# A Mamba and mixture-of-experts layer: block 0's front over more PSUM banks, tables by stage, normalisation on ScalarE

## What is computed

```python
xn = (x - mean(x)) / sqrt(var(x) + 1e-5)
# state-space layer: E = 512 channels, N = 16 states
hidden, gate = split(xn @ W_in)
hidden = silu(conv4(hidden) + conv_bias)          # causal, depthwise
dt, B, C = split(hidden @ W_x)                    # 128, 16, 16 columns
dts = softplus(dt @ W_dt + b_dt)
state = exp(dts * A) * state + dts * B * hidden   # scan over the tokens
y = (sum_n(state * C) + hidden * D) * silu(gate)
out1 = y @ W_out
# experts: 32 of them with 96 columns, all computed, weighted by the top 8
rw = top8(softmax(xn @ router.T)), divided by its sum
out2 = sum_e((silu(xn @ w_gate[e]) * (xn @ w_up[e])) @ w_down[e] * rw[e])
out = x + out1 + out2
```

## Time and profile before

| | |
|---|---|
| median of 3 runs | 1367.48 us (1365.01 to 1369.09) |
| the profiled run | 1367.53 us, its span 1365.7 us |
| TensorE busy, products and weight loads | 1312.0 us (96%), 1233.5 us (90%) |
| VectorE busy | 1242.2 us (91%) |
| ScalarE busy | 1193.1 us (87%) |
| GpSimd busy | 1243.7 us (91%) |
| mean granted TensorE clock | 0.995 |

### The profile page before, as it was taken

One profiled execution on the slowest core, in us unless ns is written; L12 is line 12 of the kernel. 1 busy time (PEld: TensorE's weight loads), 2 busy tenths in 40 slices (PEclk: granted clock), 3 DMA queues, 4 the chain that ended last, 5 costly groups with the idle time before them and its releaser, 6 DMA issues.

```text
span 1365.7 us, 26543 instructions
## 1 busy us (share of the span) xinstructions
PE 1312.0 (96%) x9314; PEld 1233.5 (90%) x9314; DVE 1242.2 (91%) x1644; ACT 1193.1 (87%) x1990; POOL 1243.7 (91%) x625
## 2 busy tenths in 40 slices
PE   2599999999999999999999999999999999999998
PEld 2589999999999999999999999999999999999987
DVE  4598989999899999999999899999989999998987
ACT  3889899889889988999899989989998999988984
POOL 2789999999989999999999999999999999999996
PEclk9899999999999999999999999999999999999999
DMA  6544344534434544444444434434443444434442
GB/s 167 153 133 122 118 130 126 129 115 128 128 113 127 140 121 122 127 119 122 124 125 129 123 114 123 144 115 129 121 124 115 130 131 127 121 119 118 124 133 70
DMA packets 184533, 170.76 MB, mean 125 GB/s; under 512 B 42672, under 2 KB 167632, under 8 KB 184400
## 3 DMA queue, kind: packets, MB, share of 16 engines
q1 hardware_dynamic: 150608, 121.86, 30.7%
q10 hardware_dynamic: 33792, 47.20, 12.1%
HBM read 163.72 MB, written 5.24 MB: 124 GB/s over the span
## 4 chain that ended last, share of the span: by engine, by line
PE 53%; DVE 16%; POOL 12%; ACT 9%; issue 9%; ACTq 1%; SPq 0%; DMA 0%; DVEq 0%; POOLq 0%
PE pair_ps L849 22%; PE out_ps L967 12%; PE front_ps L849 7%; POOL state L468 6%; DVE state L750 5%; PE turn_ps L929 5%; PE out_ps L977 3%; ACT decay L546 3%; DVE acc L757 3%; POOL state L477 3%; POOL moe L483 2%; DVE u L767 2%; ACT L546 2%; DVE dt L738 2%; DVE moe L774 1%
## 5 line engine op out<-in xcount | busy, mean ns | idle before, releaser
L750 DVE TENSOR_TENSOR_SCAN state<-decay,state 128x512 f32<-128x512 f32 x512 | 615.0, 1213 | 70.6 <-ACT decay L546 67.4
L468 POOL TENSOR_TENSOR state<-du,b_rep 128x1024 f32<-128x1024 f32 x256 | 639.2, 2505 | 29.0 <-DVE u L767 28.9
L546 ACT ACTIVATE decay<-dt,neg_a 128x255 f32<-128x255 f32 x1024 | 437.2, 467 | 39.6 <-DVE state L750 27.2
L967 PE MATMUL out_ps<-w_down,moe 128*128 128x256 f32 x1536 | 353.0, 379 | 0.1
L483 POOL TENSOR_TENSOR moe<-moe,rw_rep 128x512 f32<-128x512 f32 x192 | 285.9, 1492 | 45.8 <-DVE moe L774 36.5
L967 PEld LDWEIGHTS out_ps<-w_down,moe 128*128 128x128 f32 x1536 | 283.1, 190 | 34.6 <-issue 0.5
L849 PE MATMUL pair_ps<-xnT_hi,w_up_hi 128*128 128x256 f32 x768 | 228.7, 298 | 8.9 <-ACT moe L554 8.7
L477 POOL TENSOR_TENSOR state<-state,c_rep 128x1024 f32<-128x1024 f32 x96 | 228.6, 2382 | 2.7 <-DVE state L750 2.7
L546 ACT ACT_TABLE_LOAD x176 | 225.8, 1283 | 3.1
L849 PE MATMUL pair_ps<-xnT_hi,w_gate_hi 128*128 128x256 f32 x768 | 223.2, 291 | 0.6 <-DVE moe L774 0.5
L849 PE MATMUL pair_ps<-xnT_hi,w_up_lo 128*128 128x256 f32 x768 | 217.6, 283 | 0.0
(11 more groups left out here) (112 smaller groups left out, 2055.2 us busy)
## 6 DMA issues: line engine op xcount, KB each, us to landing
w_down<-in_L_ffn_w_down_dram SPq DMA_DIRECT2D x384, 128.0 KB, 2.6
b_rep<-b_dram ACTq DMA_DIRECT2D x128, 256.0 KB, 3.4
rw_rep<-rw_dram SPq DMA_DIRECT2D x256, 96.0 KB, 2.6
rw_rep<-rw_dram SPq DMA_DIRECT2D x256, 64.0 KB, 2.7
c_rep<-b_dram ACTq DMA_DIRECT2D x96, 128.0 KB, 3.1
rw_rep<-rw_dram SPq DMA_DIRECT2D x256, 32.0 KB, 2.5
x_in<-L_attn_input_states_dram SPq DMA_DIRECT2D x16, 256.0 KB, 3.5
res<-L_attn_input_states_dram SPq DMA_DIRECT2D x16, 256.0 KB, 4.1
```

The costliest lines, as they stand in the source:

```text
L468: pool.tensor_tensor(state[:, n % STATES, :, :], du2[:, q, :, :], b_rep[:, n // BCH % 2, n % BCH, :][:, None, :].broadcast_to([P, ET, T]), ...
L546: last = act.activation(decay[:, h, j, 1:T], dt[:, q, e, 1:T], ACT.Exp, scale=neg_a[:, e, n:n + 1])
L750: dve.tensor_tensor_scan(x, decay[:, h, :, :].rearrange("p e t -> p (e t)"), x, 0.0, ALU.mult, ALU.add).then_inc(scanned, 1)
L967: last = pe.matmul(out_ps[:, c, :], moe[:, p % RING, j, c * P:(c + 1) * P], w_down[:, p % RING, j, :], start=(p == 0 and j == 0 and c == 0 ...
```

## The change

Five things are altered together.

1. In block 0 the front's products are spread: `hid1`, `lowT` and `dt1` go to the first half of `turn_ps`, `logits` and `weightsT` to the second; both are idle before the first scan. `hid1` then no longer waits for `taps0`, nor `dt1` for ScalarE's reading of `dt0`. The router's two steps are no longer in `FRONT` and have semaphores of their own in all blocks. In block 0 `low` doesn't wait for them; in the others it still waits for `weights_read`.
2. `w_in` is split by columns, the hidden half as split 0, the gate half as split 13. `hid0` waits for split 0 alone.
3. The tables have three stages: block 0, blocks 1 to 14, and block 15.
4. VectorE's `normed` becomes one small instruction, `shift` = -mean * rstd, and two passes of ScalarE (`normed`, Identity with scale and bias). A wait is added: ScalarE's `normed` for `shift_ready`.
5. The last product of `route` (weights divided by their sum) becomes `share`, two passes of ScalarE, which wait for `rw_step`.

The diff also lets VectorE take some of GpSimd's `weigh` and `state_output` steps, but the lists that choose them are empty; these steps keep their engine, and their semaphores are renamed.

```diff
-    FRONT = ["xnT", "hid0", "hid1", "logits", "weightsT", "low", "lowT", "dt0", "dt1"]
-    BY_SCALAR = [name for name in FRONT if name not in ("xnT", "logits")]
+    FRONT = ["xnT", "hid0", "hid1", "low", "lowT", "dt0", "dt1"]
+    ROUTER = ["logits", "weightsT"]
+    BY_SCALAR = FRONT[1:]
...
-    PE_FRONT = {'xnT': -112, 'hid0': -106, 'hid1': -99, 'logits': -90, 'weightsT': -59, 'low': -56, 'lowT': -46, 'dt0': -44, 'dt1': -24}
-    SILU_AT = [-4, 13, 26, 36, 44, 55, 62, 73, 94, 94, 113, 113]
-    SCALAR_FRONT = {'xnT': -115, 'hid0': -108, 'hid1': -93, 'weightsT': -64, 'low': -54, 'lowT': -51, 'dt0': -40, 'dt1': -29}
-    CONV_SILU_AT, ROUTER_EXP_AT, SOFTPLUS_AT, FIRST_AT, SKIP_AT = [-66, -71, -22, 6, 18]
+    def stage(i):
+        return 0 if i == 0 else 2 if i == BLOCKS - 1 else 1
+    UNIT_AT = [[-30, -19, -12, -11, -8, 16, 23, 31, 36, 48, 55, 60, 66, 66, 76, 78, 85, 90, 103, 103, 107, 110, 122, 123],
+               [2, 4, 8, 17, 19, 21, 27, 44, 45, 47, 48, 65, 65, 71, 72, 84, 85, 85, 104, 106, 110, 112, 120, 120],
+               [-5, 1, 10, 26, 27, 28, 37, 37, 43, 46, 55, 55, 65, 65, 69, 69, 84, 97, 101, 115, 142, 144, 165, 175]]
+    PE_FRONT = [{'xnT': -126, 'hid0': -118, 'hid1': -99, 'logits': -95, 'weightsT': -14, 'low': -68, 'lowT': -57, 'dt0': -56, 'dt1': -39},
+                {'xnT': -112, 'hid0': -111, 'hid1': -102, 'logits': -87, 'weightsT': -52, 'low': -49, 'lowT': -46, 'dt0': -42, 'dt1': -29},
...
+    SILU_AT = [[-14, -13, 20, 28, 37, 52, 65, 67, 97, 99, 116, 116],
+               [-1, 14, 24, 39, 46, 55, 60, 73, 96, 97, 116, 119],
+               [-3, 27, 36, 37, 57, 59, 69, 70, 85, 93, 130, 232]]
+    SCALAR_FRONT = [{'xnT': -119, 'hid0': -116, 'hid1': -100, 'weightsT': -9, 'low': -76, 'lowT': -74, 'dt0': -58, 'dt1': -55},
...
+    SCALAR_ALONE = [{'conv_silu': -84, 'router_exp': -79, 'softplus': -20, 'first_state': 14, 'skip': 7, 'normed': -120, 'share': -17},
+                    {'conv_silu': -75, 'router_exp': -81, 'softplus': -22, 'first_state': 7, 'skip': 20, 'normed': -124, 'share': -63},
+                    {'conv_silu': -82, 'router_exp': -80, 'softplus': -19, 'first_state': 6, 'skip': 16, 'normed': -123, 'share': -68}]
...
+    VECTOR_ALONE = [{'stats': -121, 'lo': -87, 'logits': -54, 'route': -48, 'taps0': -61, 'taps1': -57, 'total': 163, 'shift': -118},
+                    {'stats': -126, 'lo': -107, 'logits': -78, 'route': -60, 'taps0': -97, 'taps1': -89, 'total': 163, 'shift': -121},
...
-    SPLIT_SCALAR_AT = [-116, -115, -102, -91, -86, -84, -79, -77, -61, -60, -49, -38, -31, -25, -17, -5, 1, 12]
+    SPLIT_SCALAR_AT = [-123, -100, -95, -81, -81, -76, -74, -58, -26, -24, -17, -11, -3, 0, 4, 4, 6, 8]
...
-        splits = [(w_in[0][:, k, :], w_in[1][:, k, :], w_in_d[k * P:(k + 1) * P, :]) for k in range(HT)]
+        w_in_rows = w_in_d.rearrange("(k p) e -> p k e", p=P)
+        splits = [(w_in[0][:, :, 0:E], w_in[1][:, :, 0:E], w_in_rows[:, :, 0:E])]
...
+        GATE_SPLIT = 1 + (WGROUPS - 1) * 2 * HT
+        splits.insert(GATE_SPLIT, (w_in[0][:, :, E:2 * E], w_in[1][:, :, E:2 * E], w_in_rows[:, :, E:2 * E]))
...
+        def front_bank(i, name):
+            if i == 0 and name in ("hid1", "lowT", "dt1"):
+                return turn_ps[:, 0, :].rearrange("p (j t) -> p j t", j=2)
+            if i == 0 and name in ROUTER:
+                return turn_ps[:, 1, :].rearrange("p (j t) -> p j t", j=2)
+            return front_ps
+        def weights_rows(i):
+            return acc[0:X, 1, 0:T] if i == 0 else rwT
...
+            def share(i):
+                act.wait_ge(rw_step, 3 * i + 3)
+                if i > 0:
+                    act.wait_ge(weights_filled, i)
+                for c in range(TT):
+                    last = act.activation(rw[:, c, :], rest[:, c, :], ACT.Copy, scale=inv[:, c:c + 1])
+                last.then_inc(rw_ready, 1)
+            def normed(i):
+                act.wait_ge(shift_ready, i + 1)
+                for c in range(TT):
+                    last = act.activation(x_in[:, c, :], x_in[:, c, :], ACT.Identity, bias=shift[:, c:c + 1], scale=rstd[:, c:c + 1])
+                last.then_inc(xn_ready, 1)
...
-            def normed(i):
+            def shifted(i):
                 dve.wait_ge(rstd_ready, i + 1)
-                for c in range(TT):
-                    last = dve.tensor_scalar(x_in[:, c, :], x_in[:, c, :], moments[:, c, 0:1], rstd[:, c:c + 1],
-                                             ALU.subtract, ALU.mult)
-                last.then_inc(xn_ready, 1)
+                dve.scalar_tensor_tensor(out=shift[:, :], in0=moments[:, :, 0], scalar=-1.0, in1=rstd[:, :],
+                                         op0=ALU.mult, op1=ALU.mult).then_inc(shift_ready, 1)
...
-                dve.wait_ge(rw_step, 3 * i + 3)
-                if not (isinstance(i, int) and i == 0):
-                    dve.wait_ge(front_filled, filled(i - 1, "weightsT"))
-                dve.scalar_tensor_tensor(out=rw[:, :, :], in0=rest[:, :, :], scalar=1.0,
-                                         in1=inv[:, :, None].broadcast_to([P, TT, X]), op0=ALU.mult, op1=ALU.mult).then_inc(rw_ready, 1)
...
                     if name == "hid0":
                         pe.wait_ge(front_read_v, i + 1)
-                        if first_pair(i):
-                            wait_split(pe, HT)
-                    else:
+                        if i == 0:
+                            pe.wait_ge(split[0], 1)
+                    elif i > 0:
                         pe.wait_ge(taps_done, 2 * i + 1)
...
                 elif name in ("dt0", "dt1"):
-                    pe.wait_ge(front_read_a, read_a(i, "lowT" if name == "dt0" else "dt0"))
+                    pe.wait_ge(front_read_a, read_a(i, "dt0" if name == "dt1" and i > 0 else "lowT"))
```

291 lines of the change are left out of this document (186 added, 105 removed).

## The result

The changed kernel takes 1372.57 us in the median of 7 runs (1371.39 to 1373.78) against 1367.48 of 7 runs before (1365.01 to 1369.19): a ratio of 1.0036, 95% interval [1.0024, 1.0048]. It is slower by a third of a per cent. The forecast was 1352.5 in 1338 to 1365. The profiled run took 1371.6 with a span of 1369.8, against 1367.53 and 1365.7.

What follows compares the result with a forecast made beforehand. It took TensorE to be at most about 1 us from its floor per period, with the chain passing through VectorE. 1367.5 - 8 (block 0) - 5.6 (middle) - 1.5 (end) = 1352.4, stated as 1352.5, range 1338 to 1365.

Steps and rivals of the forecast that it cites:

- (a) to (e): Block 0's front, link by link: `hid0` at 13.2, `conv_silu` 22.8, softplus 37.2, first scan 46.0, 8.7 us gained.
- Paid back in block 0: Block 0 behind its first scan: leftover splits cost each queue time; gain taken as 8 us, between 6.3 and 11.6.
- The middle: The 14 periods: net -0.6 on VectorE's stretch, -0.4 a period taken because of TensorE's floor, -5.6 us in all.
- the new order of everything else: Middle periods: reordering the remaining steps was taken at zero, with +/-0.7 us a period as bounds.
- the cost of ScalarE's queue: Middle: `normed` ahead of `first_state` and state 2's decay makes VectorE wait for the decay, 0.8 us a period.
- `shift` at 0.8: Middle: time that `shift` adds on VectorE per period, 0.8 us within bounds of 0.2 and 1.46.
- The relief of VectorE: Middle: VectorE loses `normed` and the last router product, 2.2 us, less `shift`: 1.4 us a period, between 0.8 and 2.0.
- "`share` ... no cost.": Middle: `share` waits for routing on ScalarE; VectorE has 2.4 us of work before needing the decay behind it, so no cost.
- The floor of TensorE: Each period: TensorE's counted work is 80.5 us of 81.4, at most about 1 us to gain whatever the order.
- Rival 3: ScalarE's queue (`normed`, `first_state`, state 2's decay) costs more than it frees: period up by 1.0, 1372.5 us, chance 0.07.
- The end: The last block's own tables move pair work behind the scans: -1.5 us, from -3.5 to +1.5.
- rival 1: Only the front counts: `shift` costs 1.46, the middle stays at 81.4 a period; 1358.5 us, chance 0.25.

Runs made afterwards that it cites:

- `shift_late`: Changed kernel with `shift` and `normed` in blocks 1 to 15 moved behind the two scans of state 1: 1367.76 us, ratio 1.0007.
- `mid_before_vec`: Changed kernel with blocks 1 to 14 in the old order and, in all blocks, normalisation and router scaling on VectorE: 1397.99 us, period 81.11.
- `old_normed`: `hybrid` with the normalisation alone put on ScalarE in the middle blocks, behind `shift` on VectorE: 1383.23 us, period 82.61.
- `share_vec`: `shift_late` with the router's scaling back on VectorE: 1385.81 us, ratio 1.0140, period 83.42.
- `end14`: `front_seam` with block 15 from slot 0 in the new last order and block 14's tail in the new middle order: 1357.64 us, ratio 0.9930.
- `pool_shift`: `shift_late` with `shift` computed by GpSimd behind `rstd`, in two small products: 1366.66 us, ratio 0.9999, period 82.03.
- `silu_early`: `shift_late` with pair 1's silu in blocks 1 to 14 moved ahead of `first_state` and state 2's decay: 1460.16 us, period 88.8.
- `pool_old`: `shift_late` with the old order for GpSimd's `weigh` and rowmul and VectorE's `rowadd` in the middle blocks: 1454.92 us, ratio 1.0644.
- `front_seam`: Old order except fronts of blocks 0 and 1; blocks 0 to 2 normalise and scale on ScalarE, `shift` on GpSimd; block 0's tail as before: 1357.90 us.
- `hybrid`: New order for fronts of blocks 0 and 1 and block 15's scans; otherwise old order with both steps on VectorE: 1366.14 us, ratio 0.9997.

## Why the prediction was wrong, step by step

**The front, (a) to (e): right.** `hid0` at 13.69 (13.2 predicted), `conv_silu` 23.02 (22.8), `low` 24.22 with 4.61 (23.95, 4.64), softplus 37.05 (37.2), first scan 45.28 (46.0).

The forecast kept 4.64 for `low` because TensorE would be at its low level. In the rows of before the granted clock reads 1.00 from 35 to 40 and so doesn't show it; in after the same 16 products took 4.61 us at a granted 0.50 (24 to 29), against 2.17 at 1.00 in the steady state.

**Paid back in block 0: the size was right, partly by luck, and the list was not complete.** I counted splits per queue and took 8, total 151. `shift_late` has that total, 151.2. Two things it was made of were off in opposite ways: its first scan came at 44.5 instead of 46.0, and VectorE's low parts behind it took 2.42, 0.94 and 2.66 us against a single one of 1.43 before, 4.6 more instead of the 2.4 counted. What I left out is that block 1's `shift` and `normed` are part of block 0's slots and were moved too, `shift` in front of a scan. I had priced `shift` in the middle only, where GpSimd's `rstd` is done early; in block 0 GpSimd reaches `rstd` at 51.01, behind `du`, state inputs and a split. That cost 6.0 us, part of it TensorE's 11.7 us of waiting (7.6 in `shift_late`) and its low level after it. The sentence on what would make the prediction wrong named GpSimd's queue as the way to lose the lead, and so it was, through a wait on VectorE.

**The middle: here the prediction failed.** It priced the two moved steps by themselves (-0.6, taken -0.4) and took the new order of everything else "at zero, with +/-0.7 a period". That second step is the one that failed. With the steps on VectorE the new order costs 3.7 a period; the move then gives 2.7 back. Taken the other way round, the move costs 2.1 and the order gives 1.2 back. Order and engine had to be priced together. Their sum is +0.6 in after against before, and +0.9 against `mid_before_vec`, whose 81.11 is the old order with the new kernel's semaphores. Of the parts:
- The wait was sought at the wrong engine. I put the cost of ScalarE's queue at 0.8 of VectorE waiting for the decay. That was worked out for the new order, where `first_state` and the decay of state 2 stand behind `normed`; there VectorE's wait for decays fell from 42.0 to 21.8 us in ten periods, and TensorE waits 7.4 for the silu in that queue and 7.2 for GpSimd's `weigh`. In `old_normed` the wait for decays grows by 0.8 a period (41.7 to 49.6 in ten), but there those two steps stand in front of `normed`, so the agreement is luck.
- `shift` at 0.8 was low: 1.12 in after and 1.44 in `old_normed` (14.4 us for ten), inside the range of 0.2 to 1.46. The two passes of `normed` take 1.09 instead of 0.9, those of `share` 0.52 instead of 0.45.
- The relief of VectorE was taken from the old order, where the last router product costs 0.22. In the new order it costs 2.28 there (`share_vec`), and moving it gains 1.2 a period.
- "`share` ... no cost." In after that holds, TensorE never waits for it. In the old order it doesn't: TensorE's transpose of the weights waits 1.0 us in each block, and the period is 0.76 longer.

The floor of TensorE, 80.5 by count, was not contradicted: no run's period came below 81.09.

**Rival 3 has the number, 1372.5, and that is luck.** Its place is in the chain (`normed`, `first_state`, decays, the displaced silu with its table load, 960 to 967), and the 7.4 us that TensorE waits for that silu are on record. But its sum had +1.0 a period and the whole front kept, where +0.6 and a front short of 6 us were measured. And its claim, that ScalarE's queue costs more than the move frees, holds in the old order only; in the new one the steps are 2.7 a period dearer on VectorE. It had a chance of 0.07. I had argued against it with VectorE's two scans as cover; they cover the decay and nothing else in that queue.

**The end:** -1.6 by the scans against -1.5, -3.5 by the totals. By the same cut it is -0.7 in `end14` and nothing in `pool_shift`, so the agreement to a tenth means little.

**Long and short durations of small instructions.** `shift` took 0.15 us in one place, 2.28 in another, 1.12 on average; the long ones end with a GpSimd instruction, as the pair at 52.3 does, and so does the scaling of `share_vec`. The Trainium skill, GPSIMD Engine Reference, section Key points, says that GpSimd shares its SBUF interfaces with VectorE and contends with instructions of two SBUF inputs: the traces agree. They don't show that such an instruction always waits, as the prediction read it: it depends on where GpSimd is. Had I taken the upper bound of 1.46 for `shift`, the forecast would have been rival 1's middle, nearer to the truth by 0.4 a period.

**What stays open.** In after TensorE waits for silu and for `weigh`, but why both come late in the new order no run shows, so why its period is 82.0 and not lower stays open. `pool_shift` excludes `shift`; `silu_early` and `pool_old` changed more than they should have. GpSimd's longer wait for `rowadd` and the 1926 ns of that instruction were not separated from the order. Nor is it settled why the old order runs at 81.42 in before and 81.1 to 81.2 in `front_seam` and `hybrid`; single periods take values near 81.0 and 81.5 in both.

## What to carry to other kernels

An order written out by hand and the assignment of its steps to engines are one setting: price a moved step by everything that stands behind it in its new queue up to the next engine that reads any of it, not by the first reader alone. A lead gained at the start has to be followed through the first steps that belong to the next stage, and through each seam where one order hands over to another; here a two-element instruction in front of a scan, with the two passes that wait for it, took 6 us, and a projection ahead of its neighbour up to 2.9. On VectorE a small instruction can last as long as what GpSimd is doing: look at its duration in the order in which it will stand. Judge an order change per period on the chip before adding it to others.

## What the hardware showed

- A VectorE instruction on 128x2 elements with two SBUF inputs took 0.15 us between GpSimd's instructions and up to 2.28 us beside one; one on 128x64 0.22 us in before and 2.28 in `share_vec`, beside a GpSimd product. `u<-u,state` (128x1024, two SBUF inputs) took 1446 ns on average in `hybrid`, 1577 in before and 1926 in after, different orders of the same work.
- In after ScalarE needs 588 ns (median; 583 to 601, 32 times) for 128x256 from SBUF to SBUF with a bias and a scale per partition, against 498 in the earlier trace rows for the same shape with a scale alone.
- After 11.7 us without a product TensorE was granted 0.50, the 1.2 GHz level, from 60 to 70 us in after. In `shift_late`, with a gap of 7.6 us that ended at 56.55, it was granted 0.50 from 55 to 60 and 0.93 from 60 to 70.
